# A graph-attention layer on one core: more ones products at TensorE's start, b1's dot products ahead of the first transposes

## What is computed

```python
h = jnp.maximum(_layernorm(x, axis=-1), 0.0)
h = h @ W1 + b1
e = leaky_relu((h @ a1)[:, None] + (h @ a2)[None, :] + b2, 0.2)
attention = softmax(where(adj > 0, e, -1e12), axis=1)
return x + elu(attention @ h)
```

## Time and profile before

| | us |
|---|---|
| median of 3 runs | 424.5 |
| lowest, highest run | 424.14, 427.58 |
| span of the profiled execution | 422.2 |
| median of the runs less that span | 2.3 |
| TensorE busy / weight loads busy | 416.1 / 409.9 |
| DVE busy | 374.3 |
| ACT busy | 309.0 |
| first projection starts (chain) | 12.14 |

### The profile page before, as it was taken

One profiled execution on the slowest core, in us unless ns is written; L12 is line 12 of the kernel. 1 busy time (PEld: TensorE's weight loads), 2 busy tenths in 40 slices (PEclk: granted clock), 3 DMA queues, 4 the chain that ended last, 5 costly groups with the idle time before them and its releaser, 6 DMA issues.

```text
span 422.2 us, 8433 instructions
## 1 busy us (share of the span) xinstructions
PE 416.1 (99%) x3325; PEld 409.9 (97%) x3325; DVE 374.3 (89%) x404; ACT 309.0 (73%) x306; POOL 24.9 (6%) x44
## 2 busy tenths in 40 slices
PE   8999999999999999999999999999999999999996
PEld 7888899999999999999999999999999999999996
DVE  4897999999998499999995699999992999999955
ACT  4689898999983778867664879768574789586622
POOL 1021100000000400000000400000001200000003
PEclk9999999999999999999999999999999999999999
DMA  8950068555557446648388066657477166566302
GB/s 268 392 214 0 2 212 339 199 200 199 199 200 255 145 166 233 206 147 297 112 308 302 25 205 241 248 146 258 148 260 284 71 231 207 193 224 260 114 3 98
DMA packets 22585, 82.40 MB, mean 195 GB/s; under 512 B 1531, under 2 KB 14113, under 8 KB 14242
## 3 DMA queue, kind: packets, MB, share of 16 engines
q1 hardware_dynamic: 22276, 81.81, 54.8%
q10 hardware_dynamic: 286, 0.27, 0.2%
HBM read 77.86 MB, written 4.21 MB: 194 GB/s over the span
## 4 chain that ended last, share of the span: by engine, by line
PE 96%; DVE 2%; DMA 1%; ACT 0%; issue 0%; ACTq 0%; DVEq 0%
PE ps L771 53%; PE ps L773 27%; PE ps L652 5%; PE ps L793 2%; PE ps L794 2%; PE ps L795 2%; PE ps L640 2%; DMA v_rows<-vectors 1%; DVE adj_s L879 1%; DVE h_raw L864 0%; PE ps L595 0%; PE ps L605 0%; DVE y L1086 0%; PE ps L747 0%; PE ps L621 0%; PE ps L612 0%
## 5 line engine op out<-in xcount | busy, mean ns | idle before, releaser
L773 PE MATMUL ps<-hp_lo,w_hi 128*128 (+1 forms) x936 | 226.8, 282 | 0.0
L771 PE MATMUL ps<-hp_hi,w_hi 128*128 (+1 forms) x936 | 226.8, 282 | 0.0
L879 DVE SCALAR_TENSOR_TENSOR adj_s<-R,p,adj_s 128x1024 f32<-128x1024 f32 x128 | 165.2, 1330 | 24.2 <-ACT adj_s L450 24.0
L771 PEld LDWEIGHTS ps<-hp_hi,w_hi 128*128 128x128 f32 x936 | 176.8, 189 | 0.0
L773 PEld LDWEIGHTS ps<-hp_lo,w_hi 128*128 128x128 f32 x936 | 176.7, 189 | 0.0
L458 ACT ACTIVATE w_hi<-adj_s 128x2048 fp32r<-128x2048 f32 x64 | 122.4, 1912 | 37.5 <-DVE adj_s L879 37.2
L889 DVE SCALAR_TENSOR_TENSOR w_lo<-adj_s,w_hi 128x2048 fp32r<-128x2048 f32 x64 | 145.9, 2280 | 0.0
L450 ACT ACTIVATE adj_s<-adj_s 128x2048 f32<-128x2048 int32 x64 | 122.3, 1910 | 25.9 <-DMA adj_s<-adj_t 25.8
L771 PE MATMUL ps<-hp_hi,w_lo 128*128 (+1 forms) x944 | 123.0, 283 | 0.0
L771 PEld LDWEIGHTS ps<-hp_hi,w_lo 128*128 128x128 f32 x944 | 117.3, 189 | 0.0
L652 PE MATMUL ps<-W1x,hnT 128*128 128x258 f32 x128 | 30.2, 382 | 0.0
(11 more groups left out here) (110 smaller groups left out, 188.6 us busy)
## 6 DMA issues: line engine op xcount, KB each, us to landing
adj_s<-adj_t SPq DMA_DIRECT2D x64, 1024.0 KB, 4.9
x_s<-x SPq DMA_DIRECT2D x7, 512.0 KB, 8.8
o_s<-x SPq DMA_DIRECT2D x3, 1024.0 KB, 7.6
out<-o_s SPq DMA_DIRECT2D x6, 512.0 KB, 6.8
R<-r_rows SPq DMA_DIRECT2D x1, 1536.0 KB, 6.4
adj_s<-x SPq DMA_DIRECT2D x1, 1024.0 KB, 5.5
out<-adj_s SPq DMA_DIRECT2D x8, 128.0 KB, 1.7
x_s<-x SPq DMA_DIRECT2D x2, 256.0 KB, 3.8
```

What stands on the lines that cost most here:

```text
L771: last = pe.matmul(acc, block_w, hh, start=fresh, stop=False)
L773: pe.matmul(acc, block_w, hl, start=False, stop=False)
L879: last = dve.scalar_tensor_tensor(sgn, R[:, ds(ic * CW, CW)], p[:, ds(source(r, c) + s, 1)], sgn, ALU.max, ALU.mult)
```

## The change

`WARM` has four numbers now: eleven products of ones at the start (six before), two behind `turn_W1`, five behind `weigh_b1`, and two behind `weigh`. `turn_W1` follows `spread_b1` at once. `weigh_b1` stands ahead of `transposes(0)`; it waits for the kept vectors and b1rep (`acol_kept`) instead of the first relu, and writes to bank 6 instead of bank 1, still two columns wide. The wait for its copy, `ba_kept`, moves from ahead of `transposes(2)` to ahead of `transposes(1)`, which write to that bank. On ACT, `keep_ba` stands ahead of `relu_T(0)`, and `keep_wv` ahead of `root(1)`.

```diff
-WARM = (6, 2, 1)
+WARM = (11, 2, 5, 2)
...
+        BB = 6
...
-                act.activation(ba[:, :], ps[:, SB, 0:2], ACT.Copy).then_inc(ba_kept, 1)
+                act.activation(ba[:, :], ps[:, BB, 0:2], ACT.Copy).then_inc(ba_kept, 1)
...
             keep_WT()
+            keep_ba()
             relu_T(0)
+            keep_wv()
             root(1)
-            keep_wv()
-            keep_ba()
             normalise(1)
...
-                pe.wait_ge(hn_ready, KC)
+                pe.wait_ge(acol_kept, 4)
                 for c in range(KC):
-                    pe.matmul(ps[:, SB, 0:2], b1rep[:, c, :], acol[:, A1:A2 + 1, c], start=c == 0, stop=False)
-                pe.matmul(ps[:, SB, 0:1], ones[0:1, 0:P], v_row[0:1, 3 * F:3 * F + 1], start=False, stop=True).then_inc(ba_ps, 1)
+                    pe.matmul(ps[:, BB, 0:2], b1rep[:, c, :], acol[:, A1:A2 + 1, c], start=c == 0, stop=False)
+                pe.matmul(ps[:, BB, 0:1], ones[0:1, 0:P], v_row[0:1, 3 * F:3 * F + 1], start=False, stop=True).then_inc(ba_ps, 1)
...
             spread_b1()
+            turn_W1()
             keep_warm(WARM[1])
-            turn_W1()
+            weigh_b1()
             keep_warm(WARM[2])
             transposes(0)
             weigh()
-            weigh_b1()
+            keep_warm(WARM[3])
             pe.wait_ge(w1x_ready, 1)
             project(0, 0)
+            pe.wait_ge(ba_kept, 1)
             transposes(1)
...
-            pe.wait_ge(ba_kept, 1)
```

## The result

| | before | after |
|---|---|---|
| median of 22 runs, us | 426.2 | 423.12 |
| lowest, highest run | 423.46, 428.65 | 422.70, 423.81 |
| span of the profiled execution | 422.2 | 421.8 |
| TensorE busy in it | 416.1 | 416.8 |
| first projection starts in it | 12.14 | 12.02 |

The ratio of the times is 0.9928, with a 95% interval from 0.9907 to 0.995. The median lies inside the stated range (422.9 to 425.3), 1.0 us under the 424.1 forecast.

What follows compares the result with a forecast made beforehand. TensorE, busy 416.1 of 422.2 us, was taken to bound the kernel, at its lower clock level early on. Span 422.2 less 0.4 gained plus 2.3 around it gave 424.1 us, range 422.9 to 425.3.

Steps and rivals of the forecast that it cites:

- Parts (a) to (e): TensorE's start: added ones products and new order put the first projection at 11.77 us instead of 12.14, 0.4 gained.
- (b): TensorE behind the starting ones: vectors, b1's spreading, stall, W1's transposes, two ones products; 3.35 us at the lower clock.
- Part (f): ACT's root(1) behind keep_wv: root(1) moves from 11.08 to 11.6 us, DVE by 0.5, eating most of its first reserve.
- The time: Whole kernel: profiled span 422.2 less 0.4 gained plus 2.3 us around the span gives 424.1 us.
- Rival 3: Kernel's start: before's slow profiled start was chance, its rise usually at 8.7 us; 424.5 to 425.0 us, chance 0.12.
- The 5.4 us of unbroken work: TensorE's unbroken work before the clock rose in before's trace, carried over to put the rise at 6.4 us.
- Rival 1: TensorE's start: filled gap brings an early rise (4.4 to 5.5 us); 0.8 to 1.3 us gained, 423.4, chance 0.22.
- Rival 2: TensorE's start: late rise, from 7.15 us on added ones cost more than they give; 425.2 us, chance 0.13.
- Rival 4: ACT or DVE takes over: root(1) late by 0.5 us or more, reserves used up, gain stops; 424.5, chance 0.13.

Runs made afterwards that it cites:

- e1_fill: The kernel before with eleven ones products at the start in place of six, nothing else changed; median 423.44 us.
- e5_notail: The changed kernel without the two ones products behind W1's products with a; 12 runs from 422.69 to 423.74 us, median 423.35.

## Why the prediction was right, and where it was not

The range held the median, for a reason that was only half mine.

- Parts (a) to (e), with the rise carried over to 6.4 us, gave 9.59 us for the transposes, 10.46 for W1·a, 11.34 for the last ones and 11.77 for the projection. Measured: 9.81, 10.68, 11.47 and 12.02, with the rise at about 6.2. The 0.2 us are the sum of larger misses that partly cancel, which is luck. The 22 passes end at 6.04, not 5.67 (the first row had shown it: twelve passes in 2.93 us, not the 2.56 that 0.213 us each would give); 0.14 us of that is left at 7.85, since the rise came 0.2 us sooner than assumed and nearly all of (b) ran at the upper level. b1's products then took 0.65 us in place of 0.81, the ten passes behind them 1.31 in place of 1.07 (here a stall stands that the sum had left out), W1·a 0.79 in place of 0.88, the last ones 0.55 in place of 0.43. The gain at the projection's start is 0.12 us, not 0.4; another 0.19 us that I did not foresee comes from the projection itself, 1.75 in place of 1.94, which no longer follows a one-row product at once. That this is why is my reading and isn't shown: e1_fill keeps that neighbour and takes 1.94 too, but in e5_notail, where the projection waits for ACT and follows no one-row product, it takes 2.01. So the 0.4 us of the spans is the forecast size for a reason that is only in part the forecast one, and that is luck.
- Part (f) held closely: root(1) at 11.57 (11.6 said), ACT's second normalisation at 12.30 (12.3), the reserve at 21.11 gone, the gain through to the end of the prologue.
- The step that failed is "The time": 422.2 - 0.4 + 2.3. The 2.3 is the median of three runs less the span of one execution. In every run on record that has both numbers, time less span is 1.7 to 1.9 us (423.61 less 421.8 for the profiled run of the changed kernel), so the profiled execution of before would count about 424.0 us, and less 0.4 gives 423.6, which is what the changed kernel's profiled run took. The same step took that execution as the typical run. That execution is near the lower group; over 22 runs the median of before is 426.2, 1.7 us higher. The three runs shown held the hint, 427.58 beside 424.14 and 424.50, and I called it scatter.
- That the median of the changed kernel, 423.12, still lies in the range is luck, too: the low end was made for a rise at 4.4 us in the changed kernel. The median is 0.5 us under the changed kernel's own profiled run, and no second trace of that kernel was taken. In the traces of other kernels with eleven products in front the rise came from 4.7 to 6.3 us (once at 13.9), against 6.2 in its own, so an earlier rise in most of its runs would fit; that is argued, not shown.
- Rival 3 asked whether the profiled start was chance, and looked only one way: an earlier rise, at 8.7. The chance lay on the other side, a rise at 18.9. The 5.4 us of unbroken work that I carried over is not a constant either. In the profiled upper execution of before 13.5 us pass from 5.32 to the rise, with no idle time but with 2.9 us of products of one or two columns (1.50, 0.85, 0.51) in them.
- Rival 1 named the mechanism of the larger gain, the filled gap, but priced it at 1.3 us from the early rise of one execution. Its value is the lost upper group: 4 us in half the runs or more.
- Rival 2 is real with the gap kept (median 426.03), and not in the changed kernel. Rival 4 did not come, though DVE's first reserve went to zero.
- The weighing of the Trainium skill's rule on transposes ("TensorE: Matmul & The Clock Gate", Part 4) came out as the row had it: against the rule, 64 transposes kept the clock at 1.00. What behaves as that rule says is the two-column product, of which the row at 10.45 in the earlier trace rows had given no sign. Part 1 of the same page of the Trainium skill, which calls the onset run-variable, agrees with the runs here, but the variation was 8.4 us of onset and about 4 us of time, not the few tenths that I took.

Open: why the upper group holds half of the runs on one chip and nearly all on another; whether the idle gap or the number of products in front decides; why the five products behind b1's go with no late rise, and three or none with some, though TensorE's instructions are the same up to there; and whether the place of b1's products adds to what the ones products give.

## What to carry to other kernels

A profile is one execution: where a kernel starts with small, gapped TensorE work, look at the single runs first, and if they fall into groups, get a profile from each before pricing a change. Fill the start of TensorE without a gap, and put full-width products before and between products of a few columns. The mean granted clock of the single runs tells a fall from a late rise without a profile. The gain is in the runs that would have lost the clock, not in the one that kept it. Count the cover against what it delays: five products guard the clock here, three do not in a third of the runs, and each costs 0.2 us (two passes of 0.107) where TensorE doesn't wait for something else.

## What the runs showed of the hardware

- Products of two columns, back to back and with their weight loads, read as fully busy and let the granted clock fall from 1.00 to 0.50 after 2.7 us of them (12.42 to 15.1). At the lower clock 17 us passed before it rose again, 8.5 of them with such products, the rest with ones, transposes, W1·a's products of two columns (1.50 us) and the projection.
- 64 transposes of 128x128, 7.15 us, left it at 1.00.
- TensorE's stream of instructions that is the same up to 10.28 us saw the clock rise at 6.2 us in one execution and at 13.9 in another; the kernel before at about 10.5 and 18.9.
- The column of the granted clock prints 1.00 from the start of a trace although the durations are those of half speed. Before the first rise only durations tell: 333 ns or 192 ns for a weight load, 0.22 or 0.11 us for a transpose. The mean of a run, 0.999 for the upper execution of before with its rise at 18.9 us and 0.990 for the one that fell from 9.4 to 16.2, has the same blind spot.
